# A fused attention and mixture-of-experts layer: the low part of the expert up weights computed on DVE instead of POOL

## The chip, the cores and the metric

The kernel runs on one core of one Trainium2 chip. The metric is the device time in microseconds of one execution; three runs of the kernel before give a median of 886.43 us (883.74 to 887.36). The engines are named as in the profile: PE is TensorE (PEld its weight loads), DVE is VectorE, ACT is ScalarE, POOL is GpSimd and SP is SyncE, which only issues DMAs here.

## What is computed

Four sequences of 1024 steps with 128 features each are normalised; the layer adds to its input an attention branch and a mixture of experts, both of the normalised input `xn`. Cut to what matters:

```
xn = layernorm(x)                                   # 4 x 1024 x 128
# attention branch: projections, causal convolution of 4 taps, silu, then a delta rule in chunks of 32:
q, k, v = silu(conv(xn @ Wq)), silu(conv(xn @ Wk)), silu(conv(xn @ Wv));  beta = sigmoid(xn @ Wb)
att = inverse of (I + strictly lower triangle of (k*beta) @ k.T), per chunk and head;  u = att @ (v*beta);  w = att @ (k*beta)
for chunk i:  u_adj = u_i - w_i @ S;  o_i = q_i @ S + local @ u_adj;  S = S + k_i.T @ u_adj
fir_s, fir_l = causal filters of 3 and 31 taps over v
p = gates(gelu([xn, fir_s, fir_l, o] @ Wf1 + bf1) @ Wf2 + bf2)
attn = rmsnorm(p0*fir_s + p1*fir_l + p2*o + p3*v) @ Wo
# experts: each token takes the best 2 of 8
z = (xn @ W1_e + b1_e) * (xn @ W2_e + b2_e)         # 128 -> 256, "up"
g = z @ Wg_e + bg_e;  h = g * sigmoid(g) * (z @ Wl_e + bl_e)     # 256 -> 256, "mid"
y_e = h @ W3_e + b3_e                               # 256 -> 128, "down"
out = x + attn + sum over the two chosen e of weight_e * y_e
```

The products with `W1`, `W2`, `Wg` and `Wl` are made with split operands: a float32 value is a high part (rounded to float32r by a copy) and a low part (the value minus its high part), and `a @ b` is `ah @ bh + ah @ bl + al @ bh`, three matmuls.

## The kernel before

**Attention** goes through 8 windows of 128 steps of the four sequences. Per window there are projections into a shared PSUM bank (`project`), the convolution (`conv0` on ACT, three `conv` steps on DVE, line 1392), `gate` and `silu` (line 1401), transposes and norms (`gate_T`, `sumsq`, `normed`, `q_T`, `k_T`), the triangular systems (`products`, `masks`), which go through DRAM to another layout (`system`, `solve_in`), are inverted on DVE by 15 steps of a product and a sum (`solve_mul`, `solve_sum`, lines 1466 and 1472), and come back (`inverse_out`, `inv`); then the recurrence over four chunks (`on_state`, `u_adj`, `state`, `o`), the filters (`fir`, line 1498, and `fir_l`), the gates (`fuse` to `blend`) and the mix (`fir_s_T` to `rms`, `o_T`, `out`, `store`).

**Experts** are run on tiles of 512 slots, 23 tiles in all, once the tokens have been sorted to experts (`choose`, `count`, `place`; then `mark`, `owned` and `own` make the lists of rows, lines 1355 to 1375). For each tile t:

- `load_split` (SP, line 852) loads the up and mid weights of the tile's expert, 768 KB, into the one buffer `w_split`. It waits until both low parts of tile t-1 are made (semaphores `up_low` and `mid_low`).
- `split_up`: ACT copies the up weights (columns 0 to 511) to `w_up` as their high part (line 1103) when the load has landed; POOL then subtracts it from `w_split` to make the low part (line 1036) and signals `up_low`. `w_up` has two buffers.
- `split_mid`: ACT copies the mid weights (1024 columns, line 1108), once the last matmul of tile t-1 has read `w_mid`, which is one buffer; DVE makes their low part (line 1293).
- `load_xs` (POOL) gathers the tile's token rows by four indirect DMAs (line 1031); `turn` and `split` turn them round and split them into `xr`.
- `up1`, `up2` (PE into `ps_x`; the trace also shows them by line 1625, the helper `product`) wait for `up_low`. `z` multiplies them (DVE, line 1591), ACT makes its high part (line 1246) and POOL its low part (`zlow`, line 1076).
- `mid_g`, `mid_l`, `swish` and `times` (DVE, lines 1595 and 1600), `down` (PE, line 1850), `y_out` (DVE, line 1605), and `y_put`: POOL scatters the rows by four indirect DMAs (line 1042).

After the last tile `fetch`, `combine` and `give` bring the two expert rows of each token to the output.

**Order of the work.** Nothing is decided at run time: each engine goes through one list of steps, in order, and waits on semaphores. `plan()` makes the five lists beforehand. It is a list scheduler over some forty streams of steps. `FLOW` says for each step which engines it takes, in phases, with an assumed busy time; among the steps that could start within `NEAR` = 0.5 of the earliest one, the one with the greatest rank is taken, where the rank is the assumed length of what still follows it, plus a number per name (`PULL`), plus a number per name times the window or tile number (`LEAN`):

```python
starts.append((max(ready[n], clock[engine]), tails.get(last[n], 0.0) + PULL.get(last[n][0], 0.0)
               + LEAN.get(last[n][0], 0.0) * last[n][1], n))
first = min(starts)[0]
best = max((s for s in starts if s[0] <= first + NEAR), key=lambda s: (s[1], -s[0]))
```

So a step on another engine, or another number in these tables, can move steps on all engines. What an engine's list says is binding: if the step at its head waits, all behind it wait too.

## Time and profile before

| | |
|---|---|
| median of 3 runs | 886.43 us (883.74 to 887.36) |
| the profiled execution, device time | 884.17 us |
| its span, first to last instruction | 882.4 us |
| mean granted clock of TensorE | 0.842 |
| busy: PE, DVE, POOL, ACT | 658.0, 568.8, 458.6, 299.6 us |
| HBM traffic | 45.35 MB read, 17.56 MB written |

A time in the rows is in us from the span's start unless ns is said. A row of the timeline gives the start, the duration, the engine, the line and the operation (out<-in) with its shape and a count, and in brackets how long the engine had been idle before it and what ended that. Sorting and marking take the time up to about 115 us, the experts run from there to about 820 us with the attention windows between them, and the last window ends the program.

### The profile page before, as it was taken

Reading aid. Unit: us, or ns where it says so; the run is one execution under the profiler, and the core shown is the slowest. Engines: PE = TensorE matmul, PEld = TensorE weight load, DVE = VectorE, ACT = ScalarE, POOL = GpSimd, SP = SyncE. Lnnn points to the kernel's source line nnn. Section 1 sums busy time; section 2 is a strip of 40 time slices with the busy share of each in tenths; the row PEclk is TensorE's granted clock in tenths of the full one; section 3 lists DMA queues with packets and bytes.
Section 4 is the critical chain, followed back from the end, with each engine's and each line's share of the span. In section 5 each row is a group of like instructions: output and inputs, shape, how many; then the busy total and the mean of one; then the engine's idle time right before and its main releaser. Section 6 shows DMA issues by size and latency. Waiting matters only on the chain.

```text
span 882.4 us, 31011 instructions
## 1 busy us (share of the span) xinstructions
PE 658.0 (75%) x13276; PEld 502.2 (57%) x13276; DVE 568.8 (64%) x1233; ACT 299.6 (34%) x519; POOL 458.6 (52%) x519
## 2 busy tenths in 40 slices
PE   2434856877687878878898686978878788899772
PEld 2223845666465656566666555666566646676651
DVE  6888957536747865965577546864477748533573
ACT  2221024323343425342254334333433343334230
POOL 3730168634826754676475755387435662723323
PEclk9985567989887968997899898898889798999775
DMA  7221121323113214131332204131324311310350
GB/s 290 107 96 54 61 54 39 105 64 86 26 39 78 64 32 114 39 77 53 88 108 64 77 14 108 44 92 38 54 61 74 69 38 45 93 53 31 107 196 12
DMA packets 62488, 64.92 MB, mean 74 GB/s; under 512 B 39824, under 2 KB 47888, under 8 KB 62224
## 3 DMA queue, kind: packets, MB, share of 16 engines
q1 hardware_dynamic: 54880, 46.84, 17.8%
q0 software_dynamic: 5888, 12.07, 6.1%
q10 hardware_dynamic: 1584, 4.04, 1.2%
q8 instruction: 105, 1.72, 0.8%
q14 instruction: 31, 0.25, 0.1%
HBM read 45.35 MB, written 17.56 MB: 71 GB/s over the span
## 4 chain that ended last, share of the span: by engine, by line
PE 29%; issue 21%; POOL 20%; DVE 18%; DMA 6%; ACT 3%; SPq 3%; DVEq 0%; POOLq 0%; ACTq 0%
PE ps_shared L1629 5%; PE ps_shared L1850 4%; POOL y_d L1042 4%; POOL xs L1031 3%; PE ps_g L1625 3%; PE ps_l L1625 3%; PE ps_x L1625 3%; DVE acc L1392 3%; PE ps_shared L1767 3%; POOL sumsq L996 2%; SPq L881 2%; DMA system_d<-masked 2%; DVE solve_prod L1466 2%; PE ps_shared L1625 2%; POOL ssq_o L1068 2%
## 5 line engine op out<-in xcount | busy, mean ns | idle before, releaser
L1042 POOL DMA_INDIRECT y_d<-work,put_i x92 | 92.3, 1004 | 80.5 <-DVE work L1605 57.4
L1031 POOL DMA_INDIRECT xs<-xn_d,owner_i x92 | 94.7, 1030 | 60.2 <-issue 24.6
L1625 PE MATMUL ps_x<-xr,w_up 128*128 128x512 f32 x276 | 98.4, 476 | 17.9 <-issue 12.0
L1076 POOL TENSOR_TENSOR z<-work,z 128x512 fp32r<-128x512 f32 x46 | 60.4, 1314 | 59.5 <-ACT z L1246 59.3
L1625 PE MATMUL ps_g<-z,w_mid 128*128 128x512 f32 x276 | 83.2, 441 | 4.6 <-POOL z L1076 4.2
L1625 PE MATMUL ps_l<-z,w_mid 128*128 128x512 f32 x276 | 82.2, 436 | 1.7 <-issue 1.1
L1392 DVE SCALAR_TENSOR_TENSOR acc<-pre,late_sb,acc 128x512 f32<-128x512 f32 x72 | 59.9, 832 | 26.9 <-ACT acc L1139 25.6
L1625 PEld LDWEIGHTS ps_x<-xr,w_up 128*128 128x128 f32 x276 | 54.8, 218 | 36.5 <-issue 18.9
L1850 PE MATMUL ps_shared<-w_plain,work 128*128 128x128 f32 x368 | 58.2, 323 | 18.1 <-DVE work L1600 13.3
L1466 DVE TENSOR_TENSOR solve_prod<-solve_T,solve_L 128x1 f32<-128x1 f32 (+14 forms) x120 | 49.4, 412 | 28.7 <-DMA solve_L<-system_d 25.3
L1850 PEld LDWEIGHTS ps_shared<-w_plain,work 128*128 128x128 f32 x368 | 53.9, 232 | 22.6 <-issue 16.5
L1625 PEld LDWEIGHTS ps_g<-z,w_mid 128*128 128x128 f32 x276 | 55.6, 210 | 18.4 <-issue 5.5
L1625 PEld LDWEIGHTS ps_l<-z,w_mid 128*128 128x128 f32 x276 | 52.2, 201 | 14.6 <-issue 2.3
L1595 DVE SCALAR_TENSOR_TENSOR work<-ps_g,w_plain,work 128x512 f32<-128x512 f32 x46 | 34.3, 746 | 31.1 <-ACT work L1252 31.1
L1036 POOL TENSOR_TENSOR w_up<-w_split,w_up 128x512 fp32r<-128x512 f32 x23 | 29.8, 1298 | 41.7 <-ACT w_up L1103 41.5
L1252 ACT ACTIVATE work<-ps_g,w_plain 128x512 f32<-128x512 f32 x46 | 31.4, 683 | 55.0 <-PE ps_g L1625 54.9
L996 POOL TENSOR_TENSOR sumsq<-sumsq,minus_half 128x16 f32<-128x16 f32 x16 | 47.6, 2975 | 1.3
L1600 DVE SCALAR_TENSOR_TENSOR work<-ps_l,w_plain,work 128x512 f32<-128x512 f32 x46 | 34.1, 741 | 21.2 <-PE ps_l L1625 20.8
L1238 ACT ACTIVATE work<-ps_x,w_plain 128x512 f32<-128x512 f32 x46 | 31.5, 684 | 47.9 <-PE ps_x L1625 41.4
L1591 DVE SCALAR_TENSOR_TENSOR work<-ps_x,w_plain,work 128x512 f32<-128x512 f32 x46 | 33.9, 737 | 19.4 <-PE ps_x L1625 18.2
L1246 ACT ACTIVATE z<-work 128x512 fp32r<-128x512 f32 x46 | 28.8, 627 | 50.4 <-DVE work L1591 50.3
L1669 PE MATMUL ps_g<-work,z 128*128 128x92 f32 x128 | 28.9, 425 | 13.0 <-DVE work L1365 13.0
(252 smaller groups left out, 1420.7 us busy)
## 6 DMA issues: line engine op xcount, KB each, us to landing
w_split<-expert_split SPq DMA_DIRECT2D x23, 768.0 KB
w_plain<-expert_plain SPq DMA_DIRECT2D x23, 196.0 KB
xa_d<-xr SPq DMA_DIRECT2D x8, 512.0 KB, 2.6
xa<-xa_d SPq DMA_DIRECT2D x8, 512.0 KB, 4.0
system_d<-masked SPq DMA_DIRECT2D x8, 256.0 KB, 2.9
x_res<-hidden SPq DMA_DIRECT2D x8, 256.0 KB, 2.8
xs<-xn_d,owner_i POOLq DMA_INDIRECT x92
y_d<-work,put_i POOLq DMA_INDIRECT x92
```

Source lines behind the costliest of these rows:

```text
L996: pool.tensor_tensor(flat, flat, minus_half[:, :], ALU.pow).then_inc(S["rnorm"], 1)
L1031: pool.indirect_dma_start(xs[par][:, c, :], None, xn_d.rearrange("w p (c d) -> (w p c) d", c=CPW), bass.IndirectOffsetOnAxis(owner_i[:, w ...
L1042: pool.indirect_dma_start(y_d, bass.IndirectOffsetOnAxis(put_i[:, w * CPW + c:w * CPW + c + 1], 0), y_sb[par][:, c * D:(c + 1) * D], None) ...
L1076: pool.tensor_tensor(low[:, :], up1[i], high[:, :].bitcast(FP), ALU.subtract).then_inc(S["z_low"], 1)
L1392: made = dve.scalar_tensor_tensor(runs(acc), pre[:, :, k:k + CHUNK], conv_w[:, n, k:k + 1], runs(acc), ALU.mult, ALU.add)
L1466: seq.mark(dve.tensor_tensor(prod, solve_T[:, 0:i, 0:i], over(solve_L[:, i, 0:i].unsqueeze(1), P, i, i), ALU.mult))
L1591: dve.scalar_tensor_tensor(up1[i], ps_x2[:, :], bias_of(1, w, i), up1[i], ALU.add, ALU.mult).then_inc(S["z"], 1)
L1595: dve.scalar_tensor_tensor(o, ps_g[:, :], bias_of(2, w, i), o, ALU.add, ALU.mult).then_inc(S["t"], 1)
L1600: dve.scalar_tensor_tensor(o, ps_l[:, :], bias_of(3, w, i), o, ALU.add, ALU.mult).then_inc(S["o"], 1)
L1625: made = pe.matmul(to, weights[a], x[b], start=start and n == 0, stop=stop and n == 2)
L1629: return pe.matmul(to[head_rows(h), at:at + n], weights, x, start=start, stop=stop, tile_position=(HD * h, HD * h), skip_group_check=True)
L1850: made = pe.matmul(ps[:, c * D:(c + 1) * D], gated[par][k][:, c * P:(c + 1) * P], down_of(w, k), start=k == 0, stop=k == FJ - 1)
```

## The change

`split_up` goes to DVE in its second phase: in `FLOW`, in the order lists that follow from it, and in the code of the two engines. The instruction itself and its wait and signal are the same. `PULL` and `LEAN` also get other numbers, in 21 places; of them a line of each stands here.

```diff
-    ... "split_up": [[(ACT_, 0.65)], [(POOL_, 1.4)]], "split_mid": [[(ACT_, 1.1)], [(DVE_, 1.9)]],
+    ... "split_up": [[(ACT_, 0.65)], [(DVE_, 0.75)]], "split_mid": [[(ACT_, 1.1)], [(DVE_, 1.9)]],
...
-PULL = {"beta_T": -200, "blend": -600, "choose": 400, "combine": -250, "conv0": 50, "count": -200, "delta_T": 50,
+PULL = {"beta_T": -200, "blend": -600, "choose": 400, "combine": -250, "conv0": 350, "count": -200, "delta_T": 150,
...
-LEAN = {"beta": -30, "beta_T": 45, "blend": 45, "combine": -15, "conv": -30, "delta_again": -40, "fetch": -10,
+LEAN = {"beta": -30, "beta_T": 45, "blend": 60, "combine": -15, "conv": -30, "conv0": 5, "delta_again": -40,
...
@@ block.gpsimd
-                elif name == "split_up":
-                    pool.wait_ge(S["up_high"], w + 1)
-                    pool.tensor_tensor(w_up[par][:, UPS:], w_split[:, 0:UPS], w_up[par][:, 0:UPS].bitcast(FP),
-                                       ALU.subtract).then_inc(S["up_low"], 1)
@@ block.vector
+                elif name == "split_up":
+                    dve.wait_ge(S["up_high"], w + 1)
+                    dve.tensor_tensor(w_up[par][:, UPS:], w_split[:, 0:UPS], w_up[par][:, 0:UPS].bitcast(FP),
+                                       ALU.subtract).then_inc(S["up_low"], 1)
```

The line numbers of the changed kernel are 1 higher up to the branch that POOL loses, 3 lower from there to the branch that DVE gains, and 1 higher behind it.

**First place: DVE while the row lists are made.** `z` and `work` hold the marks that PE (`owned`) multiplies into the lists, `own` begins with the row `work<-ps_g`. DVE's list before:

```order
L1293 TENSOR_TENSOR w_mid<-w_split,w_mid 128x1024
L1361 TENSOR_TENSOR z010<-number,lane_f 128x512
...
L1434 STREAM_TRANSPOSE head_vs<-gate 128x512
L1440 TENSOR_TENSOR v_b0<-head_vs,beta_all 128x512
L1361 TENSOR_TENSOR z000<-number,lane_f 128x512
...
L1455 TENSOR_TENSOR masked0<-ps_shared1,masks 128x256
L1498 SCALAR_TENSOR_TENSOR fir_s<-v_act0,late_sb,fir_s 128x512 x2
L1371 TENSOR_SCALAR work<-ps_g 128x92
```

and of the change:

```order
L1294 TENSOR_TENSOR w_mid<-w_split,w_mid 128x1024
L1290 TENSOR_TENSOR w_up0<-w_split,w_up0 128x512
L1362 TENSOR_TENSOR z010<-number,lane_f 128x512
...
L1290 TENSOR_TENSOR w_up1<-w_split,w_up1 128x512
...
L1435 STREAM_TRANSPOSE head_vs<-gate 128x512
L1441 TENSOR_TENSOR v_b0<-head_vs,beta_all 128x512
L1456 TENSOR_TENSOR masked0<-ps_shared2,masks 128x256
L1499 SCALAR_TENSOR_TENSOR fir_s<-v_act0,late_sb,fir_s 128x512 x2
L1372 TENSOR_SCALAR work<-ps_g 128x92
```

The subtractions of tiles 0 and 1 now stand between the marks; the steps `v_T` and `v_b` (`head_vs`, `v_b0`) of attention window 0, which stood between the marks, now stand behind the last of them.

**Second place: POOL and DVE at tile 6.** POOL's list before, from the scatter of tile 4 (`y_d`) to the root of window 3's sums:

```order
L1031 DMA xs<-xn_d,owner_i 128x128 x4
L986 COPY pre<-conv_halo 128x4x3
L916 COPY pre<-pre 128x12x3
L990 COPY conv_halo<-pre 128x12
L1042 DMA y_d<-work,put_i 19969x128 x4
L1036 TENSOR_TENSOR w_up<-w_split,w_up 128x512
L994 TENSOR_SCALAR sumsq<-sumsq 128x16
L996 TENSOR_TENSOR sumsq<-sumsq,minus_half 128x16
```

In the change the subtraction stands in DVE's list, inside the inversion of window 2:

```order
L1521 TENSOR_TENSOR u_adj<-hid,ps_shared 128x128
L1596 SCALAR_TENSOR_TENSOR work<-ps_g,w_plain,work 128x512
L1473 TENSOR_REDUCE solve_T<-solve_prod 128x10
L1467 TENSOR_TENSOR solve_prod<-solve_T,solve_L 128x121
L1290 TENSOR_TENSOR w_up<-w_split,w_up 128x512
L1473 TENSOR_REDUCE solve_T<-solve_prod 128x11
L1467 TENSOR_TENSOR solve_prod<-solve_T,solve_L 128x144
```

It has left its place behind four indirect DMAs and stands behind one step of the inversion.

**Third place: DVE at tiles 15 and 16.** In the change the subtraction follows the one of the mid weights of the tile before (`w_mid`, which lets the next load of `w_split` go) at a short distance:

```order
L1294 TENSOR_TENSOR w_mid<-w_split,w_mid 128x1024
L1521 TENSOR_TENSOR u_adj<-hid,ps_shared 128x128
L1565 TENSOR_TENSOR mix_part<-ps_shared,l 128x512
L1596 SCALAR_TENSOR_TENSOR work<-ps_g,w_plain,work 128x512
L1290 TENSOR_TENSOR w_up<-w_split,w_up 128x512
L1521 TENSOR_TENSOR u_adj<-hid,ps_shared 128x128
L1570 TENSOR_TENSOR mix_part<-ps_shared,p_val 128x512
L1574 TENSOR_TENSOR mix<-mix,mix_part 128x512
L1601 SCALAR_TENSOR_TENSOR work<-ps_l,w_plain,work 128x512
```

Three instructions stand between the two; behind the second one stand a step of the recurrence (`u_adj`) and the product of tile 14 that PE's `down` waits for (`work<-ps_l`).

## Rows read from the trace of the kernel before

**Rows 1.** The page, part 1: busy time, share of the span, instructions.

```profile
PE 658.0 (75%) x13276; PEld 502.2 (57%) x13276; DVE 568.8 (64%) x1233; ACT 299.6 (34%) x519; POOL 458.6 (52%) x519
```

**Rows 2.** The page, part 4: the chain that ended last, share of the span by engine.

```profile
PE 29%; issue 21%; POOL 20%; DVE 18%; DMA 6%; ACT 3%; SPq 3%; DVEq 0%; POOLq 0%; ACTq 0%
```

**Rows 3.** Waits: engine, line, what it waited for; us in total, times, longest.

```profile
POOL w_up L1036 <- ACT w_up L1103: 41.5, 7, 17.4
...
PE ps_x L1625 <- issue: 12.0, 10, 4.3
...
ACT pre L1131 <- PE ps_shared L1625: 46.5, 15, 17.8
```

**Rows 4.** The chain in order of time: start, us, what (the pieces on line 1036).

```profile
277.50 1.71 POOL w_up L1036
...
375.30 0.85 POOL w_up L1036
...
478.70 1.23 POOL w_up L1036
...
657.46 1.27 POOL w_up L1036
...
702.52 1.27 POOL w_up L1036
...
761.28 1.30 POOL w_up L1036
```

**Rows 5.** One line's instructions: ns min/median/max, first and last start, forms.

```profile
L1036 POOL TENSOR_TENSOR w_up<-w_split,w_up x23: 1251/1283/1708, 88.4 to 795.2; 128x512 fp32r<-128x512 f32 x23
...
L1401 DVE TENSOR_TENSOR gate<-acc,gate x24: 646/692/2404, 28.1 to 728.7; 128x512 f32<-128x512 f32 x24
...
L1293 DVE TENSOR_TENSOR w_mid<-w_split,w_mid x23: 1209/1216/2041, 90.3 to 805.5; 128x1024 fp32r<-128x1024 f32 x23
```

**Rows 6.** Timeline around the subtraction of tile 6, all engines.

```profile
305.59 0.62 ACT L1103 ACTIVATE w_up<-w_split 128x512 fp32r<-128x512 f32 x1
...
310.46 1.71 DVE L1466 TENSOR_TENSOR solve_prod<-solve_T,solve_L 128x225 f32<-128x225 f32 x1
310.64 1.27 POOL L1036 TENSOR_TENSOR w_up<-w_split,w_up 128x512 fp32r<-128x512 f32 x1
...
312.01 0.76 PE L1625 MATMUL ps_x<-xr,w_up 128*128 128x512 f32 x1 [4.31 <-issue]
```

**Rows 7.** Timeline of DVE where POOL's subtraction runs: first, longest, last case.

```profile
221.34 1.76 DVE L1416 TENSOR_TENSOR square<-head_v,sumsq 128x512 f32<-128x512 f32 x1 [2.52 <-POOL sumsq L996]
...
701.94 2.40 DVE L1401 TENSOR_TENSOR gate<-acc,gate 128x512 f32<-128x512 f32 x1
...
743.62 1.02 DVE L1466 TENSOR_TENSOR solve_prod<-solve_T,solve_L 128x16 f32<-128x16 f32 x1
```

**Rows 8.** Groups by line and shape on DVE: busy us, mean ns, idle before.

```profile
L1293 DVE TENSOR_TENSOR w_mid<-w_split,w_mid 128x1024 fp32r<-128x1024 f32 x23 | 29.5, 1282 | 1.6 <-ACT w_mid L1108 1.6
```

**Rows 9.** Timeline of DVE while the row lists are made.

```profile
87.48 2.93 DVE L1365 TENSOR_SCALAR work<-number,column_f,token_f 128x92 f32<-128x92 f32 x8
...
92.67 1.98 DVE L1365 TENSOR_SCALAR work<-number,column_f,token_f 128x92 f32<-128x92 f32 x8
...
95.77 3.08 DVE L1365 TENSOR_SCALAR work<-number,column_f,token_f 128x92 f32<-128x92 f32 x8
...
102.60 0.69 DVE L1440 TENSOR_TENSOR v_b<-head_vs,beta_all 128x512 f32<-128x512 f32 x1
...
113.63 0.25 DVE L1371 TENSOR_SCALAR work<-ps_g 128x92 f32<-128x92 f32 x1 [2.34 <-PE ps_g L1669]
```

**Rows 10.** Timeline from the mid weights of tile 9 to the copy of tile 10.

```profile
422.97 1.23 DVE L1293 TENSOR_TENSOR w_mid<-w_split,w_mid 128x1024 fp32r<-128x1024 f32 x1 [0.33 <-ACT w_mid L1108]
...
425.00 0.34 SPq L852 DMA_DIRECT2D w_split<-expert_split  x1
...
429.31 0.63 ACT L1103 ACTIVATE w_up<-w_split 128x512 fp32r<-128x512 f32 x1 [2.38 <-DMA w_split<-expert_split]
```

More of the change, by code:

```diff
@@ L111 @@
 }
-PULL = {"beta_T": -200, "blend": -600, "choose": 400, "combine": -250, "conv0": 50, "count": -200, "delta_T": 50,
+PULL = {"beta_T": -200, "blend": -600, "choose": 400, "combine": -250, "conv0": 350, "count": -200, "delta_T": 150,
         "delta_again": 350, "down": 200, "fetch": 100, "fir": -350, "fir_l": -600, "fir_l_half": 200, "fir_s_T": -300,
-        "fold": -250, "full": 200, "fuse": -50, "fuse2": -400, "gate": 50, "gate_T": -300, "gates": 600, "give": -550,
-        "inv": 200, "k_T": -550, "ln": -150, "load_plain": 200, "load_split": 150, "load_x": -350, "load_xs": -200,
-        "load_xt": 50, "low": 250, "mark": 50, "masks": -200, "mid_g": -100, "mid_l": -300, "mix_s": -100,
-        "mix_v": -350, "normed": 100, "o": 50, "out": 50, "own": 300, "owned": 600, "place": 100, "products": -250,
-        "project": 250, "q_T": -350, "rank": -150, "rms": -250, "solve_mul": -50, "solve_sum": -400, "split": -100,
-        "split_mid": 550, "split_qkv": 100, "split_up": 200, "store": -600, "swish": 50, "system": 400, "turn": -100,
-        "u": -150, "u_adj": 200, "u_out": -450, "up2": 600, "v_T": -100, "v_again": -200, "w_T": 200, "w_T_out": 350,
-        "x_res": 150, "xn_out": 250, "y_put": -600, "z": -50, "zeros": 100}
@@ L122 @@
-LEAN = {"beta": -30, "beta_T": 45, "blend": 45, "combine": -15, "conv": -30, "delta_again": -40, "fetch": -10,
-        "fir": -5, "fir_l_T": -25, "fir_s_T": 5, "full": 5, "fuse": -20, "fuse2": 40, "gate_T": 35, "gates": -30,
-        "give": 15, "inv": -35, "inverse_out": 10, "k_T": 25, "ln": -40, "load_x": -15, "load_xs": -5.2, "low": 30,
-        "mark": -30, "masks": -45, "mid_g": 12.1, "mid_l": -5.2, "mix_s": 10, "mix_v": 30, "norm": -35, "o_T_out": -25,
-        "owned": 10, "products": 45, "project": 5, "rank": 30, "rms": -5, "solve_in": -15, "split_mid": -3.5,
-        "state": 30, "store": 45, "sumsq": -15, "system": 25, "times": 10.4, "turn": -7.7, "u_adj": 25, "up2": -3.4,
-        "v_T": 40, "v_act": 30, "v_again": -40, "v_b": -60, "w_T": 15, "w_T_out": -30, "xn_out": -5, "y_out": -8.7,
-        "y_put": -10.4, "zlow": -15.6}
+        "fold": -150, "full": 200, "fuse": -50, "fuse2": -400, "gate": 100, "gate_T": -350, "gates": 600, "give": -550,
@@ new lines @@
+        "hid": 300, "inv": 200, "k_T": -550, "ln": -150, "load_plain": 200, "load_split": 150, "load_x": -350,
+        "load_xs": -200, "load_xt": 50, "low": 250, "mark": 50, "masks": -200, "mid_g": -100, "mid_l": -300,
+        "mix_s": -100, "mix_v": -350, "normed": -200, "o": 50, "on_state": -200, "out": 50, "own": 300, "owned": 600,
+        "place": 100, "products": -250, "project": 250, "q_T": -350, "rank": -150, "rms": -250, "solve_in": -200,
+        "solve_mul": 300, "solve_sum": -400, "split": -100, "split_mid": 550, "split_qkv": 200, "split_up": 200,
@@ new lines @@
+        "store": -600, "swish": 50, "system": 400, "turn": -100, "u": -150, "u_adj": 200, "u_out": -450, "up2": 600,
+        "v_T": -100, "v_again": -200, "w_T": 200, "w_T_out": 350, "x_res": 150, "xn_out": 250, "y_put": -600, "z": -50,
+        "zeros": 100}
+LEAN = {"beta": -30, "beta_T": 45, "blend": 60, "combine": -15, "conv": -30, "conv0": 5, "delta_again": -40,
+        "fetch": -10, "fir": -5, "fir_l_T": -25, "fir_s_T": 5, "full": 5, "fuse": -20, "fuse2": 40, "gate_T": 35,
+        "gates": -25, "gelu": 30, "give": 15, "inv": -35, "inverse_out": 10, "k_T": 25, "ln": -40, "load_x": -15,
+        "load_xt": -30, "low": 30, "masks": -45, "mid_g": 12.1, "mid_l": -5.2, "mix_s": 10, "mix_v": 30, "norm": -35,
+        "o_T_out": -25, "owned": 10, "products": 45, "project": 5, "rank": 30, "rms": -5, "silu": -30, "solve_in": -15,
+        "solve_sum": 15, "split_mid": -3.5, "state": 30, "store": 45, "sumsq": -15, "system": 25, "times": 10.4,
+        "turn": -7.7, "u_adj": 25, "up2": -3.4, "v_T": 40, "v_act": 30, "v_again": -25, "v_b": -60, "w_T": 15,
+        "w_T_out": -30, "xn_out": -5, "y_out": -8.7, "y_put": -10.4, "zlow": -15.6}
```

2 lines of the change are left out of this document (1 added, 1 removed).

## The prediction

> **What bounds the kernel now.** I read the page's busy times first: PE 658.0 us of a span of 882.4, DVE 568.8, POOL 458.6 [rows 1]. No engine is full, so no engine's load sets the time. The chain that ended last says the same: it is spread over PE (29%), "issue" (21%), POOL (20%) and DVE (18%) [rows 2]. The reader should see a kernel bound by hand-overs between engines whose lists are in order. Busy time then counts only where it lies on the chain: 20% against 52% busy means that 0.38 of POOL's work lies there, and 18% against 64% that 0.28 of DVE's does.
>
> Next come the waits. POOL stood 41.5 us in 7 places for ACT's copy of the up weights; 17.4 and 7.6 us of these are the first two tiles, before the row lists exist, when POOL has nothing else to do, so 16.5 us are left. PE's up products stood 12.0 us in 10 places behind "issue" [rows 3]; following each one back, all ten ended within 0.1 us of the end of POOL's subtraction. Tile 6 shows how: ACT's copy ended at 306.2, POOL was in four indirect DMAs until 310.6, and PE, idle for 4.31 us, began at 312.01 [rows 6]. So the moved step is a direct releaser of PE, and its price before is POOL's queue more than its own 1.28 us [rows 5].
>
> **The change part by part.** The sum goes by the profiled execution, 884.2 us; the median of the runs shown is 886.4, so that 0.5%, about what a measurement of this kernel can tell from no change, is below 882.0 or above 890.9.
>
> *a. POOL without the subtraction.* It loses 23 x 1.28 = 29.4 us of busy time [rows 5]. On the chain lie six pieces after the start, 1.71 + 0.85 + 1.23 + 1.27 + 1.27 + 1.30 = 7.6 us [rows 4]. In the changed lists nothing takes those places in POOL's queue: I take **-7.6**. The bounds are 0 (another wait is just as late) and -7.6.
>
> *b. PE's ten waits.* The subtraction on DVE has two inputs in SBUF and 512 columns, as line 1401, whose median is 0.69 us; the mid weights of twice the columns take 1.22 [rows 5]. Once DVE's list has come to it, it waits for the one DVE instruction that runs, 0.2 to 1.2 us, where POOL's queue held it 4.4 us at tile 6. At tile 6 it stands behind one product of the inversion instead of four DMAs (second place of the change). I take two thirds of the 12.0 us [rows 3] as gone, 8.0, and half of that as time, since PE and "issue" together make half of the chain [rows 2]: **-4.0**. Bounds: 0 and -12.0.
>
> *c. DVE with it.* After the marks 21 subtractions add 21 x 0.69 = 14.5 us. But POOL's subtraction cost DVE time already. A DVE instruction that meets it takes 1.0 to 2.4 us instead of its usual 0.2 to 0.75: 1.76 at 221.3, 2.40 at 701.9 (median of that line 0.69 [rows 5]), 1.02 at 743.6; these are the first, the longest and the last of twelve such after the marks, over their shapes' usual times by 12.8 us together [rows 7]. That goes. Against it DVE's new subtraction will now and then meet another POOL instruction. The nearest row is the mid subtraction, whose mean of 1.282 is 0.066 above its median [rows 5, 8]: 23 x 0.066 = 1.5 us. DVE's net is 14.5 - 12.8 + 1.5 = +3.2 us, of which 0.28 lies on the chain: **+0.9**. Bounds: 0 and +15.9, if nothing is given back and all is on the chain.
>
> The Trainium skill states the mechanism (SBUF — State Buffer, section "SBUF: two separate sides"): DVE and GpSimd share a port pair as an exclusive lock, which a DVE instruction with two SBUF inputs takes against a GpSimd instruction that reads SBUF, and the loser blocks in full. The rows above agree. By that rule the lock does not vanish, it changes sides: the moved subtraction can hold POOL back 23 x 0.69 = 15.9 us at most, where POOL's own held DVE 14.8 with the marks; if every one met a POOL read, 15.9 x 0.38 would make the sum 6 us worse.
>
> *d. The start.* While the row lists are made, DVE is the engine waited for. Two subtractions add 1.4 us; the two meetings with POOL's subtractions, at 87.5 and 95.8, where eight instructions took 2.93 and 3.08 us instead of 1.98 [rows 9], give back 2.0; and `v_T` and `v_b`, 0.7 us each, move behind the last mark (first place), into the 4.2 us between it (109.4) and `own` (113.63), of which 2.34 us were idle and which held 1.9 us of work [rows 9]; 3.3 us still fit. So `own`, for which the gather of all tiles waits, comes 2.0 + 1.4 - 1.4 = 2.0 us earlier: **-2.0**. Bounds: 0 and -2.0. DVE's second subtraction, for which a load must land, does not stop the marks: that copy ended at 97.2 in the trace, and DVE comes to it after marks that end past 98.
>
> *e. DVE's own queue stands for the copy.* What POOL did in 41.5 us DVE may now do: if its list comes to the subtraction before ACT's copy is there, all behind it waits. From the end of the mid subtraction of one tile to the end of the up copy of the next the trace has 6.3 us in the median of 22 tiles; one of the fastest is tile 10, from 424.20 by a load issued at 425.00 to 429.94 [rows 10]. I added up DVE's work between those two steps in the changed list. For 16 tiles it is 4.8 to 7.6 us, and as DVE is busy 64% of the time, the copy will mostly be there. For six (3, 10, 12, 15, 16, 22) it is 1.4 to 3.9 us; tile 15 has 0.3 + 0.7 + 0.75 = 1.7 (third place). Against 6.3 these six leave 23.5 us of standing. DVE would have been idle in 36% of that anyway, and of the rest 0.28 is on the chain: 23.5 x 0.64 x 0.28 = **+4.2**. Bounds: 0 and +23.5. Behind the standing step at tile 15 are `u_adj` of the recurrence and the product that `down` waits for.
>
> *f. The rest of the order.* The other numbers and the move rewrite all lists: of PE's 583 steps 326 keep their relative order, of DVE's 861 there are 563. The streams stay nearly level: each window's `fuse` stands within two up steps of where it stood, and from the last tile's `down` on PE's list is the same but for one exchange of neighbours. I find no reason for a sign and take **0**. The nearest measure of what one bad or good place is worth is the longest wait of the list, 17.8 us [rows 3], so I keep -17.8 and +17.8 as ends. SP is not harmed: the next load waits for both low parts, and the mid one stays the later one after the first tile.
>
> Sum: -7.6 - 4.0 + 0.9 - 2.0 + 4.2 = -8.5, and 884.2 - 8.5 = 875.7. I forecast **876 us**, 1.2% under the median.
>
> **Rivals.**
>
> *No change.* The pieces on POOL's chain are replaced by others as long, and PE, 75% busy, fills the ten gaps only to stand longer at the next product. For it: busy PE and "issue" hold half the chain, and 12.0 us are 5% of PE's idle 224. Against it: the start's 2.0 us have no such neighbour. Time: with a, b and e at 0 it is 884.2 - 2.0 + 0.9 = 883. The Trainium skill speaks for this rival (Perfetto Trace Analysis, section "Optimizing Scalar/DVE Operations"): since the two engines share an SBUF read port, moving operations between them might not help. The trace agrees on the port, and no run so far shows the rest.
>
> *DVE stands for the load, and the kernel gets slower.* One place: DVE's list at the six tiles of e. If all 23.5 us fall on the chain, because `u_adj`, `swish` and `times` stand behind, the sum is 884.2 - 7.6 - 4.0 + 0.9 - 2.0 + 23.5 = 895. It decides from 19.4 us of standing on the chain, where 890.9 is passed. For it: DVE is released by no one else, and two of the six hold the recurrence. Against it: DVE already waits in this way for ACT's mid copy, and stood only 1.6 us for it in all [rows 8].
>
> *The new order decides.* One long wait more or less, 17.8 us: 858 or 894.
>
> That the change does not do what it says is excluded: POOL's list in the change has no such step left.
>
> **How the numbers follow.** Forecast 0.56, no change 0.18, DVE stands 0.16, order 0.10 (half each way). Faster by over 0.5%: 0.52 of the forecast, 0.03 of no change, 0.05 of order make 0.60. Slower by over 0.5%: 0.12 of DVE's standing and 0.05 of order make 0.17. The rest, 0.23, is within. The forecast's own range is 868 to 882. The whole range is cut where a tenth is left at each end: below, a and b in full and part of a lucky order, 862; above, DVE's standing nearly in full, 893.
>
> **What would show it.** Right: POOL busy near 429 us; DVE busy between 565 and 580, without instructions stretched by POOL's subtraction; line 1290 at 0.69 us; `own` near 111.6; PE's waits for the up products before "issue" well under 12.0 us; the time from the end of ACT's up copy to the first up matmul near 1 us at tile 6. Wrong: a wait of line 1290 for ACT of more than some 10 us in all; `u_adj` or `times` late behind it; experts that end later than 820 us; or a POOL chain share that stays at 20%, which would mean that the subtraction was never what held it.

## The result

The changed kernel took **899.97 us** in the median of 3 runs (897.73 to 904.28), against 886.43 before: a ratio of **1.0167**, with a 95% interval of 1.0098 to 1.0237. It is slower by 13.5 us. The forecast was 876, with a range of 862 to 893, and the sign is wrong as well. The profiled execution took 899.97 us, with a span of 898.2.

### The profile page after: what moved, and what is told of

It is laid out like the page before. It is cut to its first block, busy times and chain, and to the rows that moved or that the text cites. A ratio compares the mean times of both kernels' runs of the same rounds, so it can differ in the third digit from the quotient of the medians.

```text
span 898.2 us, 31011 instructions
## 1 busy us (share of the span) xinstructions
PE 662.6 (74%) x13276; PEld 508.3 (57%) x13276; DVE 565.7 (63%) x1256; ACT 300.0 (33%) x519; POOL 432.0 (48%) x496
## 3 DMA queue, kind: packets, MB, share of 16 engines
q1 hardware_dynamic: 54880, 46.84, 17.4%
## 4 chain that ended last, share of the span: by engine, by line
PE 31%; issue 17%; POOL 14%; DVE 11%; DMA 6%; ACT 3%; SPq 2%; POOLq 0%; DVEq 0%; ACTq 0%
PE ps_shared L1630 6%; PE ps_g L1626 4%; PE ps_x L1626 4%; PE ps_shared L1851 3%; POOL xs L1032 3%; PE ps_l L1626 3%; POOL y_d L1039 3%; PE ps_shared L1768 2%; POOL sumsq L997 2%; SPq L882 2%; PE ps_shared L1635 2%; DMA system_d<-masked 2%; POOL z L1073 2%; DMA solve_L<-system_d 2%; PE ps_shared L1626 2%
## 5 line engine op out<-in xcount | busy, mean ns | idle before, releaser
L1039 POOL DMA_INDIRECT y_d<-work,put_i x92 | 95.0, 1033 | 114.2 <-DVE work L1606 91.2
L1032 POOL DMA_INDIRECT xs<-xn_d,owner_i x92 | 96.5, 1049 | 85.4 <-DVE put_i L1376 42.7
L1626 PE MATMUL ps_l<-z,w_mid 128*128 128x512 f32 x276 | 84.3, 443 | 1.0 <-DVE work L1601 0.6
L1393 DVE SCALAR_TENSOR_TENSOR acc<-pre,late_sb,acc 128x512 f32<-128x512 f32 x72 | 57.1, 793 | 39.2 <-ACT acc L1136 38.1
L1467 DVE TENSOR_TENSOR solve_prod<-solve_T,solve_L 128x1 f32<-128x1 f32 (+14 forms) x120 | 41.6, 347 | 43.4 <-DMA solve_L<-system_d 39.6
L1851 PE MATMUL ps_shared<-w_plain,work 128*128 128x128 f32 x368 | 55.7, 315 | 16.8 <-DVE work L1601 16.3
L1626 PE MATMUL ps_shared<-xa,w_qkv 128*128 128x512 f32 x72 | 27.8, 503 | 15.2 <-issue 9.8
L1789 PE MATMUL ps_shared<-head_vs,taps 32*32 32x32 f32 x2048 | 34.0, 228 | 5.8 <-issue 5.8
```

The source lines that it names most:

```text
L1032: pool.indirect_dma_start(xs[par][:, c, :], None, xn_d.rearrange("w p (c d) -> (w p c) d", c=CPW), bass.IndirectOffsetOnAxis(owner_i[:, w ...
L1039: pool.indirect_dma_start(y_d, bass.IndirectOffsetOnAxis(put_i[:, w * CPW + c:w * CPW + c + 1], 0), y_sb[par][:, c * D:(c + 1) * D], None) ...
L1393: made = dve.scalar_tensor_tensor(runs(acc), pre[:, :, k:k + CHUNK], conv_w[:, n, k:k + 1], runs(acc), ALU.mult, ALU.add)
L1467: seq.mark(dve.tensor_tensor(prod, solve_T[:, 0:i, 0:i], over(solve_L[:, i, 0:i].unsqueeze(1), P, i, i), ALU.mult))
L1626: made = pe.matmul(to, weights[a], x[b], start=start and n == 0, stop=stop and n == 2)
L1789: made = pe.matmul(by_half[rows, :, e % KH], taps[rows, e, last, :], head_vs[rows, at:at + 2 * RUNS, e], start=e % KH == 0 and not last, s ...
```

## The profile after

Busy times and the chain by engine, from the page of the changed kernel, to be set against [rows 1, 2]:

```profile
PE 662.6 (74%) x13276; PEld 508.3 (57%) x13276; DVE 565.7 (63%) x1256; ACT 300.0 (33%) x519; POOL 432.0 (48%) x496
PE 31%; issue 17%; POOL 14%; DVE 11%; DMA 6%; ACT 3%; SPq 2%; POOLq 0%; DVEq 0%; ACTq 0%
```

POOL has 26.6 us less to do and fell from 20% to 14% of the chain. DVE, which took the 23 subtractions over, is 3.1 us less busy than before. PE does the same 13276 matmuls in 4.6 us more. So the load is gone where it was meant to go, and the kernel is still 15.8 us longer from the first to the last instruction. Slower matmuls are not the reason, though the mean granted clock is lower here (0.814, before 0.842): in another profile of the same kernel (e9 below, clock 0.825, span 898.4) PE is as busy as before:

```profile
PE 658.5 (73%) x13276; PEld 505.9 (56%) x13276; DVE 561.4 (62%) x1256; ACT 300.3 (33%) x519; POOL 431.9 (48%) x496
```

The moved step itself, first as one line's instructions (ns min/median/max), then in the timeline around tile 6, where before PE had stood 4.31 us [rows 6]:

```profile
L1290 DVE TENSOR_TENSOR w_up<-w_split,w_up x23: 678/686/693, 93.0 to 798.2; 128x512 fp32r<-128x512 f32 x23
```

```profile
297.08 0.63 ACT L1100 ACTIVATE w_up<-w_split 128x512 fp32r<-128x512 f32 x1 [1.31 <-DMA w_split<-expert_split]
...
297.74 0.69 DVE L1290 TENSOR_TENSOR w_up<-w_split,w_up 128x512 fp32r<-128x512 f32 x1 [0.49 <-ACT w_up L1100]
...
298.54 0.94 PE L1626 MATMUL ps_x<-xr,w_up 128*128 128x512 f32 x3
```

ACT's copy ends at 297.71, and the first up matmul stands at 298.54, 0.8 us later, without a wait in front. That is the hand-over that the change was made for, and it works.

The waits (us in total, times, longest), those that answer to [rows 3] and those that grew:

```profile
POOL y_d L1039 <- DVE work L1606: 91.2, 14, 15.6
...
ACT pre L1128 <- PE ps_shared L1626: 53.9, 18, 19.6
...
ACT gate L1151 <- DVE acc L1393: 50.4, 18, 7.7
...
DVE solve_prod L1467 <- DMA solve_L<-system_d: 39.6, 8, 8.6
DVE acc L1393 <- ACT acc L1136: 38.1, 16, 7.0
...
DVE w_up L1290 <- ACT w_up L1100: 8.4, 7, 2.6
```

PE's up products wait behind "issue" no more (12.0 us before, no such row now), and DVE stands only 8.4 us for ACT's copy. In their place other waits are longer, and none of them touches the moved step. In the trace of before the same pairs of lines have:

```profile
POOL y_d L1042 <- DVE work L1605: 57.4, 13, 14.8
...
ACT gate L1154 <- DVE acc L1392: 34.8, 19, 3.5
...
DVE acc L1392 <- ACT acc L1139: 25.6, 13, 5.4
DVE solve_prod L1466 <- DMA solve_L<-system_d: 25.3, 8, 5.0
```

These are POOL's put of the expert rows waiting for DVE's `y_out`, ACT's `gate` for DVE's `conv`, `conv` for ACT's `conv0`, and DVE's first product of an inversion for its load. The last three are of attention's chain.

Where the time goes is seen by stages. Tile 4's `z` starts at 231.3 us before and at 231.2 after, so nothing is lost up to there. The stretch from 240 to 560 us (busy time of each engine), of before and then of after:

```profile
240.00:560.00 320.00, 259.12 (x5670) 195.09 (x5672) 205.90 (x395) 124.15 (x216) 184.79 (x194) 0.87 0.25 66
```

```profile
240.00:560.00 320.00, 253.04 (x5234) 190.31 (x5235) 194.81 (x389) 119.78 (x204) 169.30 (x182) 0.83 0.24 63
```

In the same 320 us DVE got 11.1 us less work done (third pair of columns), and PE 6.1 us less, though DVE now has more of it in its list. Inside the stretch the two kinds of work are no longer level: the expert tiles 6 and 7 are 15 and 20 us ahead of before (by the start of `z`), the inversions of windows 3 and 4 are 16.6 and 29.4 us behind, and then tile 11, whose weights SP loads only after DVE has come past window 4's first product, is 27.5 us behind. From 785 us on both are 13 to 16 us late and stay so.

Window 4's inversion shows how one place of the list looks from near. Timeline of the changed kernel:

```profile
460.54 4.69 SPq L882 DMA_DIRECT2D solve_L<-system_d  x8
...
466.91 0.16 DVE L1467 TENSOR_TENSOR solve_prod<-solve_T,solve_L 128x1 f32<-128x1 f32 x1 [6.15 <-DMA solve_L<-system_d]
466.99 0.75 DVE L1601 SCALAR_TENSOR_TENSOR work<-ps_l,w_plain,work 128x512 f32<-128x512 f32 x1
467.66 1.22 DVE L1294 TENSOR_TENSOR w_mid<-w_split,w_mid 128x1024 fp32r<-128x1024 f32 x1
467.89 3.75 PE L1851 MATMUL ps_shared<-w_plain,work 128*128 128x128 f32 x16 [5.62 <-DVE work L1601]
468.79 0.69 DVE L1402 TENSOR_TENSOR gate<-acc,gate 128x512 f32<-128x512 f32 x1
469.66 0.37 SPq L853 DMA_DIRECT2D w_split<-expert_split  x1
...
472.65 1.01 POOL L1039 DMA_INDIRECT y_d<-work,put_i  x1 [15.64 <-DVE work L1606]
```

DVE stands 6.15 us for the load of the first product of the inversion. Right behind it in the list are `times` of tile 9, the mid subtraction of tile 10 and a `gate` product. By their semaphores they were ready at 460.6, 461.8 and 462.3. PE waits 5.62 us for the first of them, SP can load the next weights only behind the second, and POOL stands 15.64 us for what comes out. Before, the same product started at 437.53 after a gap of 4.32 us.

## The experiments

All times below are beside runs of the kernel before on the same chip, in four groups, each on a chip of its own. Before had a median of 884.7 us (13 runs) in the first group, 960.8 (13) in the second, 888.4 (7) in the third and 960.9 (19) in the fourth. Only ratios are compared, and across groups with care.

Two theories stood at the start. **A**: the move is worth what steps a to e of the prediction say, and the rewritten lists, step f, lose some 2%. **B**: the lists are harmless, and the move onto DVE costs more than it brings.

### The move alone, and the lists alone

**e1_move_in_old_order.** The lists of before are kept step for step; the 23 subtractions leave POOL's list and stand in DVE's, each ahead of the first DVE step that in the trace of before started after the end of ACT's copy.

```diff
+AHEAD_OF = [
...
+def moved(order, frm, to):
...
+    order[frm] = [s for s in order[frm] if s[0] != "split_up"]
+    for t, (key, nth) in enumerate(AHEAD_OF):
+        at = [n for n, s in enumerate(order[to]) if s[:3] == key][nth]
+        order[to].insert(at, ("split_up", t, 0, None, None))
+    return order
...
-    return order
+    return moved(order, POOL_, DVE_)
```

`FLOW` keeps the subtraction on POOL, so that the planner writes the lists of before; the code of the two engines changes as in the change.

> The five lists are exactly those of the kernel before, but the 23 subtractions stand on DVE, each ahead of the first DVE step that started after ACT's up copy in the trace of before. Theory A (the rewritten order lost the time, the move itself gains what terms a to e gave, 8.5 us at most): 876 to 882, PE's waits for the up products before issue under 4 us. Theory B (the move itself costs, DVE's list or DVE's share of the port lock): 893 to 903, as the change.

**e2_new_order_on_pool.** The reverse: the lists of the change, and the subtractions in POOL's again, placed by the trace of the change in the same way (`moved(order, DVE_, POOL_)`).

> The five lists are those of the change, but the 23 subtractions stand on POOL again, each ahead of the first POOL step that started after ACT's up copy in the trace of the change. Theory A (order): 900 or more, since the new order keeps its loss and POOL's queue holds the subtraction again. Theory B (the move costs): back at 883 to 890.

Measured: e1 879.09 us (875.17 to 884.28, 10 runs), ratio **0.9935** (0.9901 to 0.997). e2 904.44 us (4 runs), ratio **1.0208** (1.0154 to 1.0261). The move alone gains in the old lists. In the new ones the change's 1.0167 stands against e2's 1.0208; their intervals overlap and the chips differ, so a gain there isn't shown. The new lists cost 2% with the subtraction on either engine. Theory B falls, and A stands.

Waits of e1 (the names of lines have moved by the table's length):

```profile
POOL y_d L1074 <- DVE work L1641: 64.0, 13, 15.0
...
ACT gate L1186 <- DVE acc L1428: 35.2, 19, 3.5
DVE solve_prod L1502 <- DMA solve_L<-system_d: 28.3, 7, 5.7
...
PE ps_x L1661 <- DVE work L1627: 6.5, 4, 2.8
DVE w_up L1325 <- ACT w_up L1135: 4.2, 7, 1.1
...
PE ps_x L1661 <- issue: 0.3, 1, 0.3
```

and of e2:

```profile
POOL y_d L1079 <- DVE work L1642: 80.2, 13, 16.3
...
ACT gate L1191 <- DVE acc L1429: 50.8, 18, 7.7
...
DVE solve_prod L1503 <- DMA solve_L<-system_d: 38.0, 8, 8.7
...
PE ps_x L1662 <- issue: 14.9, 8, 2.9
```

The two waits of attention go with the lists: 35.2 and 28.3 us in the old ones, 50.8 and 38.0 in the new. The wait of PE behind "issue" goes mostly with the subtraction's engine: 0.3 on DVE in e1 and 14.9 on POOL in e2, though e3 below, with the subtraction on DVE, has 5.0.

### Which part of the rewriting

The change rewrites the lists twice over: the planner is told of another engine and length for the subtraction, and many of its numbers are other ones. **e3_replan_old_numbers** is the change with `PULL` and `LEAN` of before:

```diff
-PULL = {"beta_T": -200, "blend": -600, "choose": 400, "combine": -250, "conv0": 350, "count": -200, "delta_T": 150,
+PULL = {"beta_T": -200, "blend": -600, "choose": 400, "combine": -250, "conv0": 50, "count": -200, "delta_T": 50,
...
```

> FLOW has the subtraction on DVE, PULL and LEAN keep the numbers of before; the planner writes the lists anew. Theory A in its plain form (any rewriting of a chosen order costs): 890 to 910, no better than the change. Theory A' (only the new numbers are bad): 876 to 884. Theory B: 893 to 903.

**e4_numbers_alone** is before, with the subtraction on POOL, and `PULL` and `LEAN` of the change.

> The subtraction stays on POOL, in FLOW too, but PULL and LEAN have the numbers of the change. Theory A in its plain form: 890 to 910. Theory A' (new numbers bad): 893 to 905. Theory B: within 0.5% of before, 882 to 891.

Measured: e3 902.26 us, ratio **1.0181** (1.0129 to 1.0233). e4 906.1, ratio **1.0216** (1.0147 to 1.0284). Each half of the rewriting costs all of it, and together they cost no more. So it isn't the one bad set of numbers. Nor is it one wait: the four named above add up to 143.1 us before and 149.6 in e1, and to 219.3 in the change, 176.4 in e3 and 191.5 in e4, and which of them grew differs from one to the next (POOL's put waits 64.3 us in e3 and 51.3 in e4, before 57.4). Two further rewritings were made to see whether any other one costs as much (second group):

**e5_other_draw**

```diff
-"zlow": [[(POOL_, 1.4)]]
+"zlow": [[(POOL_, 1.37)]]
```

> The subtraction stays on POOL and the planner keeps the numbers of before, except that it is told 1.37 us instead of 1.40 for the low part of a z tile, which carries no intention at all; that alone moves 349 of the 861 steps in DVE's list, 287 of 583 on PE, 232 of 459 on ACT and 78 of 190 on POOL. Theory L (before's lists are one lucky order among many, and any other order of this planner is about 2% worse): 900 to 907 us, ratio 1.016 to 1.024. Theory N (orders scatter evenly around before, and the two numbers sets of the change happen to be bad ones): 880 to 892, ratio 0.995 to 1.008.

**e6_solve_mul_alone**

```diff
-"solve_mul": -50
+"solve_mul": 300
```

> The subtraction stays on POOL, and of the new numbers only the largest one for DVE is taken: the pull of the inversion's products from -50 to 300 (209 of 861 steps move in DVE's list, 28 on POOL). Theory P (products that are put first stand in DVE's list waiting for their loads from memory, with ready expert steps behind, and this costs the change its 2%): 897 to 905, ratio 1.012 to 1.022, and DVE's wait of solve_prod for the load of system_d above 35 us in all (25.3 before, 39.6 in the change). Theory L (any other order): the same time but that wait near 25 to 30. Theory N: 880 to 892.

Measured: e5 994.64 us beside 960.82, ratio **1.0314** (1.0221 to 1.0408). e6 987.71, ratio **1.0229** (1.0141 to 1.0316), with DVE's wait for the load of `system_d` at 30.4 us in all, where theory P wanted over 35. An edit of 0.03 us in one cost, which means nothing, costs 3.1% on this chip, over the 1.016 to 1.024 that theory L gave. Theory N falls. P misses the mark that it set (over 35 us), but that mark was taken from traces of a faster chip, and no profile of before was taken on this one. The better argument against it is e16 below, on a chip as slow: 29.8 us of the same wait, at a cost of 0.4%. So e6's loss does not come by this wait alone; that the pull of the products causes it is not excluded. L stands, with its size too small. The lists of before are one order out of many, and a better one than the five others of this planner that were measured whole.

How much has to be rewritten was asked in the fourth group, with two small edits:

**e15_small_draw**

```diff
-"split_up": [[(ACT_, 0.65)], [(POOL_, 1.4)]]
+"split_up": [[(ACT_, 0.65)], [(POOL_, 1.3)]]
```

> The subtraction on POOL and the numbers of before, with the planner told 1.30 us instead of 1.40 for the subtraction: 13 of 861 steps move in DVE's list, 15 of 583 on PE, 9 of 459 on ACT, 6 of 190 on POOL, none on SP. If the cost grows with how much of the lists is rewritten: 0.998 to 1.004. If the lists of before are so finely set that any step out of place costs: 1.005 to 1.015.

**e16_late_draw**

```diff
-"blend": 45
+"blend": 60
```

> The subtraction on POOL and the numbers of before but one (the lean of the blend from 45 to 60): the lists are those of before up to about 538 us and rewritten behind it (143 of 861 steps on DVE, 109 on PE, 73 on ACT, 21 on POOL). If the cost grows with the share that is rewritten: 1.005 to 1.012, and not before 538 us. If the numbers of before only matter in the first half: 0.998 to 1.004.

Measured: e15 959.69 us beside 960.91, ratio **1.0000** (0.9957 to 1.0042, 10 runs). e16 964.49, ratio **1.0039** (1.0003 to 1.0075, 10 runs). A step is out of place on DVE if it is left over when the largest set of steps that both lists hold in the same order is taken out. 13 such steps cost nothing that can be seen. 125 in the second half cost 0.4%; the interval reaches into both expectations, so e16 does not decide between them. 290 to 335 over the whole length cost 1.7 to 3.1%, and e6 with 197 cost 2.3%. (The expectations have 143, 349 and 209 for e16, e5 and e6, by a matching that misses some steps.) So a large rewriting costs and a small one does not, and how the cost grows between them stays open. Where e16 loses its 0.4% can't be read off either, since its trace and e15's sway by 5 to 10 us against each other from 370 us on, ahead of the place where it rewrites.

### By what the rewritten lists lose

The timeline above suggests theory **H**: steps that are ready stand on DVE behind one that waits. The test takes the lists as they are and moves such steps ahead of the one that waits, at each place where the trace shows both. The tables name 16 steps for the new lists and 20 for the old ones, where the expectations say 17 and 21.

**e7_ready_first_new** (in the new lists):

```diff
+READY_FIRST = [
+    (('solve_mul', 2, 1), [('swish', 4, 1), ('z', 5, 0)]),
+    (('solve_mul', 3, 1), [('y_out', 6, 0)]),
+    (('full', 3, 0), [('conv', 4, 5), ('split_up', 10, 0)]),
+    (('solve_mul', 4, 1), [('times', 9, 1), ('split_mid', 10, 0), ('silu', 5, 0)]),
...
+def ready_first(order):
...
+    dve = order[DVE_]
+    for late, ready in READY_FIRST:
+        for key in ready:
+            step = dve.pop(next(n for n, s in enumerate(dve) if s[:3] == key))
+            dve.insert(next(n for n, s in enumerate(dve) if s[:3] == late), step)
+    return order
```

> The change as it is, but at the 11 places where the trace of the change shows DVE idle 3 to 8.6 us ahead of a step while 1 to 4 later steps in its list were ready, those 17 steps stand ahead of it (z, swish, times, silu, split_mid and the like, 0.7 to 1.9 us each, some 15 us of DVE work in all, into gaps of 58 us). Theory H (the change is late because ready work stands behind waiting work on DVE): 900 falls by 8 to 15, to 885 to 892. Theory S (the loss is spread over all engines' lists, and DVE's single gaps are only where it shows): it falls by less than 4, to 896 to 901.

**e8_ready_first_old** has the same function on e1's lists, with a table from e1's trace:

```diff
+READY_FIRST = [
+    (('solve_mul', 2, 1), [('fir_l_T', 0, 0), ('conv', 3, 1), ('y_out', 3, 0)]),
+    (('solve_mul', 3, 1), [('z', 7, 0)]),
...
+    (('solve_mul', 4, 1), [('v_T', 4, 0), ('times', 9, 1), ('split_mid', 10, 0), ('z', 10, 0)]),
...
```

> The old order with the subtraction moved onto DVE (879.1 us, 0.9935 of before), and the same kind of edit at the 10 places where its trace shows DVE idle with ready steps behind (21 steps moved ahead). Theory H: a further 5 to 10 us less, 869 to 874, ratio 0.982 to 0.988. Theory S: within 3 us of the unedited order, 876 to 882, ratio 0.990 to 0.997; some of the steps moved ahead now hold up the one that they passed, so a loss of up to 4 us is possible too.

Measured, on the second group's chip: e7 971.75 us, ratio **1.0111** (1.0067 to 1.0156). e8 949.87, ratio **0.9860** (0.9792 to 0.9928). Since before itself was 8.6% slower on that chip, these could not be set beside the change or e1, and all four went to one chip in the third group:

> The change unedited, beside the three others of this group, since the chip of the last group ran before 8.6% slower (960.8 us against 884.7) and its ratios can't be set beside those of the first group. Theories H and S both: 1.015 to 1.025 of before.

> The change with the 17 ready steps ahead of the waiting ones on DVE, 1.0111 of before on the slower chip. Theory H (over half of the loss is ready work behind waiting work on DVE): 1.003 to 1.010 of before here, at least 0.9% under e9. Theory S (the loss is spread over all lists): within 0.5% of e9.

> The old lists with only the 23 subtractions moved, 0.9935 of before in the first group. If the move alone is worth what it seemed: 0.990 to 0.997 again. If it was a draw of that chip: 0.998 to 1.005.

> The same lists with 21 ready steps ahead of the waiting ones on DVE, 0.986 of before on the slower chip. Theory H: 0.4 to 1.0% under e11 (0.983 to 0.989 of before). Theory S: within 0.3% of e11.

Measured, beside 888.43 us of before:

| kernel | us, median | ratio | 95% interval |
|---|---|---|---|
| e9, the change itself | 902.3 | 1.0168 | 1.0125 to 1.0211 |
| e10, its ready steps first | 896.51 | 1.0102 | 1.0043 to 1.0161 |
| e11, the move in the old lists | 879.13 | 0.9898 | 0.9848 to 0.9948 |
| e12, its ready steps first | **866.93** | **0.9774** | 0.9700 to 0.9847 |

e9 repeats the result. e11 repeats e1 (0.9935), somewhat better. The edit is worth 5.8 us in the new lists (e9 less e10) and 12.2 us in the old (e11 less e12). With four runs of each kernel the first has some 5 us of noise either way and the second some 7, so both are clear of zero, the first barely. The first figure lies between what H and S expected; the second is over what either gave. So the moving ahead of ready work is worth a good deal, but it is no answer to what the new lists lose, since the old ones have nearly as much of it. Added up over the trace from 118 us on, DVE's idle time during which one of the next eight steps of its list was ready (by its semaphores; stretches over 0.8 us) is 105.9 us before, 105.7 in e1, 118.6 in the change, 124.4 in e10 and 75.0 in e12. The count goes by one rule for when a step is ready; a looser rule gives 119, 122, 127, 132 and 91, the same picture. In the old lists the edit took 31 us of it away, in the new ones none: each gap that it filled opened another. Of the 23.2 us between e9 and e11 it takes back 5.8, and what the other 17.4 are made of stays open, beyond the waits of attention's chain named above.

The place looked at above, in e12:

```profile
428.58 0.75 DVE L1660 SCALAR_TENSOR_TENSOR work<-ps_l,w_plain,work 128x512 f32<-128x512 f32 x1 [0.42 <-PE ps_l L1685]
429.66 1.23 DVE L1353 TENSOR_TENSOR w_mid<-w_split,w_mid 128x1024 fp32r<-128x1024 f32 x1 [0.33 <-ACT w_mid L1164]
430.80 0.75 DVE L1651 SCALAR_TENSOR_TENSOR work<-ps_x,w_plain,work 128x512 f32<-128x512 f32 x1
432.80 0.80 DVE L1526 TENSOR_TENSOR solve_prod<-solve_T,solve_L 128x1 f32<-128x1 f32 x1 [1.25 <-DMA solve_L<-system_d]
```

`times`, the mid subtraction and a `z` now stand ahead of the product, whose wait is 1.25 us in place of 4.64 in e1. Over the whole kernel the wait for that load and the work done between 240 and 560 us, in e12:

```profile
DVE solve_prod L1526 <- DMA solve_L<-system_d: 13.2, 6, 3.8
```

```profile
240.00:560.00 320.00, 264.80 (x5849) 197.71 (x5838) 217.58 (x429) 127.58 (x222) 179.30 (x189) 0.88 0.26 69
```

and in e10 the same two:

```profile
DVE solve_prod L1492 <- DMA solve_L<-system_d: 15.5, 7, 5.0
```

```profile
240.00:560.00 320.00, 254.44 (x5244) 191.01 (x5243) 197.76 (x391) 120.28 (x205) 168.78 (x183) 0.84 0.25 65
```

The wait fell in both, by 24.1 us from the change's profile to e10 and by 15.1 from e1 to e12. In e12 DVE did 217.6 us of work in the stretch, more than in any other of these kernels. In e10 it did 197.8, hardly more than the change's 194.8: its gaps moved elsewhere. There ACT's wait for DVE's `conv` is still 50.2 us and DVE's for ACT's `conv0` 44.5, where e12 has 38.2 and 33.2.

A second round was read from the traces of e10 and e12 (fourth group): more steps on DVE, and on ACT as well, such as

```diff
+READY_FIRST_ACT = [
...
+    (('split_up', 5, 0), [('state', 1, 0), ('gate', 3, 0), ('mid_g', 4, 0)]),
...
```

> The lists of the change, with the 17 steps of the first round on DVE and a second round read from that kernel's own trace: 17 more steps on DVE and 18 on ACT that were ready while the engine stood idle ahead of them. Theory H (ready work behind waiting work is what the rewritten lists lose): a further 5 to 10 us less than the first round's 1.0102 of before, ratio 0.998 to 1.005. Theory S: 1.008 to 1.013, since each step that fills one gap opens the next.

> The lists of before with the move, the 21 steps of the first round on DVE, and a second round from its trace: 12 more steps on DVE and 14 on ACT. Theory H: 0.5 to 1.0% below the first round's 0.9774, ratio 0.967 to 0.973. Theory S: 0.974 to 0.981.

Measured: e13 977.06 us beside 960.91, ratio **1.0171** (1.0107 to 1.0236). e14 949.68, ratio **0.9891** (0.9829 to 0.9954). This chip is as slow as that of the second group, where the first round had given 1.0111 and 0.9860. So the second round brought nothing in either lists, and the expectation of H, 0.998 to 1.005 and 0.967 to 0.973, failed; both ratios lie above what S gave, too (1.008 to 1.013 and 0.974 to 0.981). Its table was read on a faster chip, though, and what is ready where may differ on this one. Whether it would pay on the third group's chip wasn't tried.

## Why the prediction was wrong

**The step that failed is f**, "I find no reason for a sign and take **0**". The rewritten lists cost 2.1% by e2, or 19.7 us, and by e9 against e11 23.2 us. That is past the end of 17.8 us which the prediction kept for it and gave a chance of 0.10, half each way. The rival of the new order, at 894 us, had the mechanism that came true, with too small a size and half of its 0.10 on this side. A sign there was: all five orders that were drawn anew over the whole length lost, by 1.8 to 3.1% with the subtraction left on POOL or DVE (e2 to e6; the change itself 1.7%), one of them by an edit with no meaning. Why the old one is the better is argued only: over a hundred numbers in two tables set it, and nothing but a search over them would give values such as -5.2 and 12.1. A longest single wait was also the wrong measure of what an order is worth, since lists lose by many small places: the longest of the wait that was taken as the measure is 19.6 us in the change, near the 17.8 of before, while the four waits named above grew by 76.2 us in all. The prediction's counts of steps that keep their order, 326 of 583 on PE and 563 of 861 on DVE, are too low: the longest common order has 353 and 571. Its argument does not hang on them.

**Steps a to e together** were forecast at -8.5 us. e1 and e11 gave -5.6 and -9.3 us against before's median. They hold the same move, but not all of these steps as the change has them: the subtractions stand where the trace of before had room for them, and `v_T` and `v_b` stay between the marks, so the 1.4 us of d that hang on them are not in it. The direction was right and the total near. How much of that is luck can't be said, since no run takes the terms one by one, and those that the traces show (d and e below) came smaller than forecast with opposite signs.

- *a.* POOL's busy time fell to 432.0 us, forecast near 429 (its indirect DMAs took 4.4 us more), and its share of the chain from 20% to 14%. POOL's seven waits for the copy are gone with it. The two long ones, 25 us ahead of the row lists, only became a longer wait for these: 42.7 us for `own` in place of 16.5.
- *b.* Forecast well under 12.0 us behind "issue": no such row after, 0.3 in e1. Part came back as a wait for DVE's own work in front of the same products, 1.4 us before, 6.5 in e1.
- *c.* DVE's busy time was forecast between 565 and 580: 565.7, and 569.2 in e1, where it was 568.8 before. Line 1290 takes 0.69 us, as line 1401 had said, and none of its 23 is over 0.693. DVE's other work took about as much less as the move brought: +0.4 us net in e1, where 15.9 were added. That this is the lock's return is argued from the stretched instructions of [rows 7]. The longest of these took 2.93 us, at 447.93, over two POOL instructions in a row (the subtraction and a `zlow`), and not the 2.40 that the prediction calls the longest.
- *d.* `own` was forecast at 111.6 and came at 114.7. The step held from `place` on, where DVE's row lists are made, and missed what stands before. `place` came at 76.9 in place of 74.4, by the new lists (74.7 in e1, 76.9 in e9). From there to `own` it took 37.8 us in place of 39.2, a gain of 1.4 for the forecast 2.0. In e1, without the move of `v_T` and `v_b`, the stretch from the first mark to `own` is 0.5 us shorter than before. The eight small instructions are never stretched now; these are their timeline around DVE's second subtraction, and `own`:

```profile
97.88 1.99 DVE L1366 TENSOR_SCALAR work<-number,column_f,token_f 128x92 f32<-128x92 f32 x8
99.78 0.69 DVE L1290 TENSOR_TENSOR w_up<-w_split,w_up 128x512 fp32r<-128x512 f32 x1
100.65 1.29 DVE L1362 TENSOR_TENSOR z<-number,lane_f 128x512 fp32r<-128x512 f32 x2 [0.18 <-PE ps_g L1670]
...
114.74 0.25 DVE L1372 TENSOR_SCALAR work<-ps_g 128x92 f32<-128x92 f32 x1 [0.69 <-PE ps_g L1670]
```

  The 2.93 and 3.08 us of before [rows 9] are 1.99 here, and the marks stand for PE by 0.2 to 0.5 us three times instead, which is the part that was missed.
- *e.* DVE stood 8.4 us in 7 places, longest 2.6, for the 23.5 us that were forecast at six tiles; three of the seven (tiles 12, 15 and 16, 4.5 us together) are among the six. The term was too large, and the price of what stood isn't shown by a run of its own. The rival in which DVE stands for the load came nearest in time with its 895 us, and its mechanism is not what happened: e2, where the wait is POOL's again, is no faster than the change.

**The port between DVE and POOL.** POOL's two kinds of indirect DMA, which the edit did not touch, show the lock from its other side. In e1:

```profile
L1067 POOL DMA_INDIRECT xs<-xn_d,owner_i x92 | 96.7, 1051 | 91.7 <-DVE put_i L1411 43.5 <-issue 24.6 <-PE ps_shared L1670 23.5
L1074 POOL DMA_INDIRECT y_d<-work,put_i x92 | 95.7, 1040 | 87.5 <-DVE work L1641 64.0 <-issue 23.1 <-DVE work L1627 0.3
```

They were 94.7 and 92.3 us in the trace of before. These totals do not show what the subtraction costs POOL: e11, the same kernel as e1, has 95.5 and 95.1, and e4, with the subtraction on POOL, 96.9 and 95.5. Taken one by one the instructions show it. In e1's trace 60 of the 184 began while a DVE instruction with two SBUF inputs was running, and these took 1.19 us in the mean, the other 124 took 0.97 (before: 1.13 for 53 and 0.97 for 131). Twelve of the 60 began under the moved subtraction and took 1.26 us in the mean, some 3.6 us more in all than twelve at 0.96, the usual length; the prediction gave 15.9 as the most. The Trainium skill (SBUF — State Buffer, section "SBUF: two separate sides") has the lock on both engines, and the trace agrees as to the side. The Trainium skill (Perfetto Trace Analysis, section "Optimizing Scalar/DVE Operations") also doubts that moving work between the two engines helps, because of the shared port. Against this stand e1 and e11: here it helped by 0.65 and 1.0%. That the queue which it left was worth more than the port is the likely reason; PE's wait behind "issue" (12.0 us before, 0.3 in e1) speaks for it.

## What to carry to other kernels

Where a table of numbers sets the order of all engines' lists, a change to one cost in it is two changes, and the second, a new draw of the order, can be the larger: here 2% against 1%. Make the edit in the lists as they are first, measure it, and only then draw again. And read the trace for steps that were ready behind one that waits for a load: moving 20 of them ahead, on top of the move, gave 866.9 us, 2.3% under before and the best of all kernels here.

## What the runs showed of the hardware

The chips differ by more than any edit here. Before took 884.7 and 888.4 us on two chips and 960.8 and 960.9 on two others. One kernel, e8 and e12, run on either kind shows where (PE's waits, us in total, times, longest), first on the slow chip, then on the fast:

```profile
PEld ps_shared L1689 <- issue: 104.0, 143, 6.8
...
PE ps_shared L1689 <- issue: 69.2, 81, 6.4
...
PEld ps_shared L1848 <- issue: 34.0, 51, 2.0
```

```profile
PEld ps_shared L1689 <- issue: 74.5, 90, 6.4
...
PE ps_shared L1689 <- issue: 41.3, 28, 6.0
...
PEld ps_shared L1848 <- issue: 11.7, 16, 2.0
```

These lines are groups of 1024 and 2048 matmuls of 32x32 each, and PE stands before them for nothing that the profile shows. Up to `own` at 113.5 us, where there are few of them, the two traces are level to 0.2 us, and DVE's busy time over the whole is 567.0 us on the slow chip and 570.7 on the fast. PE is also 42 us busier on the slow one (694.3 against 651.9), with a mean granted clock of 0.810 against 0.844. So what differs lies with PE, in how it starts its small matmuls and in its clock; by what, these runs don't settle. It adds to both kernels of a comparison: on either kind of chip the old lists with the ready steps first (e8, e12) are faster than before, and the new lists with them (e7, e10) slower.
